# Feed-forward weights' low parts on GpSimd, the last norm by tiles, one weight piece a slot later, and four gaps between tiles

## The reference, cut to what matters

```python
x = _layernorm(x + attn(x, Wq, bq, Wk, bk, Wv, bv, Wo, bo))   # 16 heads, 4 kv heads, rope, causal
x = _layernorm(x + wkv(w, u, x, ctx))                          # a recurrence over the rows
h = silu(x @ rw1.T + rb1)                                      # router, 64 wide
logits = (h @ rw2.T + rb2)[:, :16] + gates                     # top 2 of 16 experts, softmax
base = x @ W.T + bias
delta = einsum(einsum(x, A) * coeff, B)                        # rank 16 for each expert
x = _layernorm(x + base + delta)
```

## Time and profile before

| | |
|---|---|
| three timed runs | 1602.74, 1603.1 and 1606.97 us, median 1603.1 |
| the profiled execution | 1607.82 us, of it span 1606.0 |
| mean granted clock of TensorE | 0.991 |
| TensorE, VectorE, ScalarE, GpSimd busy | 1556.0, 1340.3, 1115.5, 1007.7 us |

### The profile page before, as it was taken

One profiled execution on the slowest core, in us unless ns is written; L12 is line 12 of the kernel. 1 busy time (PEld: TensorE's weight loads), 2 busy tenths in 40 slices (PEclk: granted clock), 3 DMA queues, 4 the chain that ended last, 5 costly groups with the idle time before them and its releaser, 6 DMA issues.

```text
span 1606.0 us, 32704 instructions
## 1 busy us (share of the span) xinstructions
PE 1556.0 (97%) x10500; PEld 1413.4 (88%) x10500; DVE 1340.3 (83%) x3434; ACT 1115.5 (69%) x2995; POOL 1007.7 (63%) x850
## 2 busy tenths in 40 slices
PE   8999999999999999999999999999999987989997
PEld 7899999999999999999999999999999976878785
DVE  6776688889888889898999889898989897877863
ACT  6777787877787778777877787878787865334332
POOL 2665586757675867676767666676667653635653
PEclk9999999999999999999999999999999999999999
DMA  9765344324442444244424442445144522121211
GB/s 298 256 225 201 112 150 137 116 73 142 150 137 55 152 146 136 60 152 151 139 60 152 151 139 60 132 146 164 44 126 148 178 70 79 53 93 66 80 66 53
DMA packets 81625, 202.62 MB, mean 126 GB/s; under 512 B 10416, under 2 KB 11056, under 8 KB 81456
## 3 DMA queue, kind: packets, MB, share of 16 engines
q1 hardware_dynamic: 81456, 200.53, 40.0%
HBM read 120.80 MB, written 37.75 MB: 99 GB/s over the span
## 4 chain that ended last, share of the span: by engine, by line
PE 84%; DVE 7%; issue 3%; POOL 2%; ACT 1%; DVEq 1%; DMA 1%; SPq 0%; ACTq 0%; POOLq 0%
PE bank L528 25%; PE bank L529 24%; PE bank L530 24%; PE bank L652 5%; PE bank L597 2%; PE bank L643 1%; PE bank L598 1%; PE bank L635 1%; DVE PS L1328 1%; DVE ED L1339 1%; PE bank L667 1%; DMA SW<-QB 1%; DVE SW L1392 0%; DVE RC L1170 0%; DVE OTl L1243 0%
## 5 line engine op out<-in xcount | busy, mean ns | idle before, releaser
L528 PE MATMUL bank<-Xh,W 128*128 128x256 f32 x1280 | 362.2, 283 | 5.8 <-DVE RC L1170 2.5
L529 PE MATMUL bank<-Xl,W 128*128 128x256 f32 x1280 | 360.5, 282 | 0.0
L530 PE MATMUL bank<-Xh,W 128*128 128x256 f32 x1280 | 360.4, 282 | 0.0
L1025 POOL TENSOR_TENSOR Ql<-RC,Qh 128x512 fp32r<-128x512 f32 x127 | 169.6, 1336 | 208.9 <-ACT Qh L744 208.7
L759 ACT ACTIVATE S<-S,NM 128x128 f32<-128x128 f32 (+1 forms) x512 | 228.2, 447 | 65.8 <-DVE NM L1155 65.2
L528 PEld LDWEIGHTS bank<-Xh,W 128*128 128x128 f32 x1280 | 241.3, 189 | 9.2 <-DVE RC L1170 5.1
L1013 POOL TENSOR_TENSOR SW<-SW,tables 128x512 f32<-128x512 f32 x128 | 170.8, 1334 | 124.6 <-DMA SW<-QB 124.5
L744 ACT ACTIVATE PTh<-bank 128x384 fp32r<-128x384 f32 x256 | 124.9, 488 | 173.1 <-PE bank L652 173.1
L529 PEld LDWEIGHTS bank<-Xl,W 128*128 128x128 f32 x1280 | 241.7, 189 | 0.0
L530 PEld LDWEIGHTS bank<-Xh,W 128*128 128x128 f32 x1280 | 241.6, 189 | 0.0
L744 ACT ACTIVATE S<-S,RL 128x128 f32<-128x128 f32 (+1 forms) x512 | 203.4, 448 | 31.7 <-DVE RL L1162 31.5
(11 more groups left out here) (161 smaller groups left out, 4450.1 us busy)
## 6 DMA issues: line engine op xcount, KB each, us to landing
W<-kept SPq DMA_DIRECT2D x140, 512.0 KB, 4.5
SW<-QB SPq DMA_DIRECT2D x256, 128.0 KB, 2.3
kept<-W SPq DMA_DIRECT2D x40, 512.0 KB, 5.0
XR<-XR SPq DMA_DIRECT2D x64, 128.0 KB, 2.3
RO<-in_xn SPq DMA_DIRECT2D x16, 512.0 KB, 4.1
KVT<-in_ctxt SPq DMA_DIRECT2D x16, 512.0 KB, 4.2
mixed<-RO SPq DMA_DIRECT2D x16, 512.0 KB, 3.8
XR<-in_xt SPq DMA_DIRECT2D x15, 512.0 KB, 4.2
```

Source lines behind the costliest of these rows:

```text
L528: nc.tensor.matmul(dst, lhs[0], rhs[0], start=first, stop=False)
L529: nc.tensor.matmul(dst, lhs[0], rhs[1], start=False, stop=False)
L530: return nc.tensor.matmul(dst, lhs[1], rhs[0], start=False, stop=last)
L1025: gp.tensor_tensor(Q[1][:, :, :], RC[:, i % 2, :, :], Q[0][:, :, :], ALU.subtract).then_inc(q_lo, 1)
```

## The change

1. Four tiles `gap0` to `gap3` that nobody uses are declared between others: 64 bytes in each partition before X, 64 before K, 64 before Q and 32 before PT. X moves by 64 bytes, K to KRC by 128, Q and S by 192, PT and all behind it by 224.
2. The low parts of the ten feed-forward pieces are subtracted by GpSimd, at the same slots, behind its own `slot(n)` and ahead of its steps.
3. Piece 8 of the first half is copied at slot 2 instead of 1, and its low part made at slot 3 instead of 2, both right ahead of piece 9's.
4. For the last batch the logits are issued in the middle part of step 17, right behind the transposes, and no longer behind `dense(1)`.
5. For the last batch the norm runs tile by tile: VectorE makes the statistics of tile 0 at the end of step 18, as soon as its sum is there, GpSimd's three operations and ScalarE's scaling are done for each tile with a semaphore count of its own, and each tile is stored by itself.

```diff
-SPLIT_AT = [[-6, -6, -2, -2, -6, -6, 0, 1, 1, 2, 3, 4] + [h // 2 + 4 for h in range(HEADS)],
+SPLIT_AT = [[-6, -6, -2, -2, -6, -6, 0, 1, 2, 2, 3, 4] + [h // 2 + 4 for h in range(HEADS)],
...
+        def gap(i, n):
+            sb(f"gap{i}", [P, n // 4])
...
+        gap(0, 64)
         X = [sb(f"X{i}", [P, 2, KC, T], fr) for i in "hl"]
+        gap(1, 64)
...
+        gap(2, 64)
         Q = [sb(f"Q{i}", [P, 2, T], fr) for i in "hl"]
...
+        gap(3, 32)
         PT = [sb(f"PT{i}", [P, 4, P + T], fr) for i in "hl"]
...
                         last.then_inc(hid_turned, 1)
+                        if f == LAST:
+                            logits()
                 else:
                     dense(1)
                     turn_x2(1)
-                    f = stage_of(n, 2)
-                    if f is not None:
...
+                    if stage_of(n, 2) != LAST:
+                        logits()
...
                         for t in range(TT):
+                            act.wait_ge(f_shift, f + 1 + t * (f == LAST))
...
-                        last.then_inc(f_done, 1)
+                            if f == LAST or t == TT - 1:
+                                last.then_inc(f_done, 1)
...
+            def ffn_weights(n):
+                for i in range(NF):
+                    if FFN_SPLIT_AT[i] + 1 == n:
+                        pool.wait_ge(w_hi, HALVES * NP + i + 1)
+                        gp.tensor_tensor(FFN_TO[i][1], ffn_stage(i), FFN_TO[i][0], ALU.subtract).then_inc(w_lo, 1)
...
                     out_sum(3, 0)
+                    if stage_of(n, 3) == LAST:
+                        dve.wait_ge(f_sum, TT * LAST + 1)
+                        dve.wait_ge(f_shift, LAST - 1)
+                        norm_stats(OUT[LAST % 2], LAST % 2, STF, MVF, VEF, f_ve, range(1))
...
-            def ffn_weights(n):
-                for i in range(NF):
-                    if FFN_SPLIT_AT[i] + 1 == n:
-                        dve.wait_ge(w_hi, HALVES * NP + i + 1)
-                        v.tensor_tensor(FFN_TO[i][1], ffn_stage(i), FFN_TO[i][0], ALU.subtract).then_inc(w_lo, 1)
```

More of the change, by code:

```diff
@@ L484, in step @@
                 if f is not None and part == 2:
-                    sp.wait_ge(f_done, f + 1)
-                    sp.dma_start(out[TAIL_BATCH[f], :, :].rearrange("(a p) c -> p a c", p=P), OUT[f % 2]).then_inc(f_out[f % 2], 16)
+                    rows = out[TAIL_BATCH[f], :, :].rearrange("(a p) c -> p a c", p=P)
+                    if f < LAST:
+                        sp.wait_ge(f_done, f + 1)
+                        sp.dma_start(rows, OUT[f % 2]).then_inc(f_out[f % 2], 16)
+                    else:
+                        for t in range(TT):
+                            sp.wait_ge(f_done, f + t + 1)
+                            sp.dma_start(rows[:, t, :], OUT[f % 2][:, t, :]).then_inc(f_out[f % 2], 16)
             def load_piece(u):
@@ L668, in turn_x2, with logits @@
                         last.then_inc(f_turned, 1)
+                def logits():
+                    f = stage_of(n, 2)
+                    if f is not None:
+                        pe.wait_ge(hid_copied, f + 1)
+                        for a in range(TT):
+                            last = nc.tensor.matmul(bank[4][:, T + a * EXP:T + (a + 1) * EXP], HST[:, a * P:(a + 1) * P], Rw2, start=True, stop=True)
+                        last.then_inc(logits_done, 1)
                 def dense(t):
@@ L1258, in odd, with norm_stats @@
                 tail(n, 0)
-            def norm_stats(tiles, par, stats, mv, ve, done):
-                for t in range(TT):
+            def norm_stats(tiles, par, stats, mv, ve, done, which=range(TT)):
+                for t in which:
                     v.bn_stats(stats[:, par, t, :], tiles[:, t, :])
                 dve.drain()
-                for t in range(TT):
+                for t in which:
                     v.bn_aggr(mv[:, par, t, :], stats[:, par, t, :])
                 dve.drain()
-                v.tensor_scalar(ve[:, par, :], mv[:, par, :, 1], EPS, None, ALU.add).then_inc(done, 1)
+                those = slice(which.start, which.stop)
+                v.tensor_scalar(ve[:, par, those], mv[:, par, those, 1], EPS, None, ALU.add).then_inc(done, 1)
             def norm_shift(par, mv, rs, nm):
@@ L1383, in step @@
                         above(dve, f_shift, f - 1)
[L1384 removed]
+                        norm_stats(OUT[f % 2], f % 2, STF, MVF, VEF, f_ve, range(f == LAST, TT))
                     f = stage_of(n, 2)
@@ L1431, in splits @@
                 v.tensor_tensor(w_part(i, 1), stages[u % STAGES], w_part(i, 0), ALU.subtract).then_inc(w_lo, 1)
-            def ffn_weights(n):
-                for i in range(NF):
-                    if FFN_SPLIT_AT[i] + 1 == n:
-                        dve.wait_ge(w_hi, HALVES * NP + i + 1)
-                        v.tensor_tensor(FFN_TO[i][1], ffn_stage(i), FFN_TO[i][0], ALU.subtract).then_inc(w_lo, 1)
-            run(dve, slot, splits, ffn_weights, step, behind=1)
+            run(dve, slot, splits, step=step, behind=1)
 def layouts(i):
```

23 lines of the change are left out of this document (10 added, 13 removed).

## The result

The changed kernel took 1589.4 us (median of four runs, 1587.6 to 1591.5) where the kernel before took 1604.7 on the same chip: ratio 0.9905, 95% interval 0.9884 to 0.9926, so 15 us less (12 to 19). In a later session the same pair gave 1588.8 against 1607.9, 0.9881 (0.9865 to 0.9898). The prediction had 6.1 us less and a range that ended at 1591. Faster was right; the size was not.

What follows compares the result with a forecast made beforehand. TensorE, busy 97% of the span, was taken as the bound, so savings elsewhere count only where it waits. Terms -1.5, -4.9, +0.3 and 0 gave -6.1: 1597.0 us from the median 1603.1, 8 in 10 range 1591 to 1603.

Steps and rivals of the forecast that it cites:

- Part 4: Address gaps before X, K, Q and PT: taken as 0, bounds 5 us less and 11 us more.
- Rival 3: Addresses help: at 1 ns per matmul on X, 5.4 us less, 1591.6 us; chance 0.12.
- Part 2: Kernel end, last batch's logits earlier and norm by tile: 4.9 us less, bounds 2.5 and 5.5.
- the clock term: Matmuls after the last weighted rows: shorter pause, no fall to 1.2 GHz, 1.6 us gained, bounds 0 and 1.7.
- The wait of the logits: Last batch's logits, issued earlier: TensorE idle 0.5 us for ScalarE's copy that they need.
- Rival 2: The clock fall before 1588 returns at another place, so the clock gain doesn't come: 1598.6 us; chance 0.15.
- Part 1: Ten low parts moved from VectorE to GpSimd: 1.5 us less, bounds 3.5 less and 1 more.
- rival 5: Low parts weren't waited for, so moving them gains 0: 1598.5 us; chance 0.06.
- the 0.3 at the hidden layer: Stop of 5.18 us at 1344.47, router's hidden layer: 0.3 us gained, bounds 1.1 gained or lost.
- I charge 0.5: GpSimd's late operations, behind pieces 8 and 9, meet two VectorE scans: 0.5 us lost, bounds 0 and 2.6.
- rival 1: GpSimd holds VectorE at the seam and delays weighted rows: Part 1 becomes +1, 1599.5 us; chance 0.17.
- Part 3: Ninth piece one slot later, near 24 us: 0.3 us more, bounds 0 and 1.1 more.

## Why the prediction was right, and where it was wrong

**What bounds the kernel: right, and it held the warning.** TensorE had no slack in the attention stage, and the text said that all else counts only "if matmuls themselves change speed". They did.

**Part 4, the gaps: the step that failed.** "One per cent lies between them, and it doesn't go with the position ... I take 0." Measured: 13 us (10 to 16) where the bound below ended at 5. Three things were wrong in it. First, compared different shapes and different pairs; X and W were in the trace at one distance only, so no row spoke about another, and the bound of 1 ns had no row under it. Nor does a rule that gives no time say that the time is nothing. Second, I read only the mean duration. It did fall with the spacing (282 to 278), but that matmuls on X could start closer together stood, before the change, only in the distances from start to start, a cycle of 112 to 124. Third, I looked for a position of each tile, modulo 128; what sorts the runs is the place of two tiles to each other. Rival 3 had the direction (the addresses help), with 1 ns on 5376 matmuls where it was 3.7 ns on 3840 and 3.3 on 1536, and a chance of 0.12. Why the distance sets the pace stays open. With 13 in its place the sum would have been 19.1: 1588.8 from the 1607.9 of the second session, which is what the changed kernel took there, and 1585.6 from the 1604.7 of the first, where it took 1589.4.

**Part 2, the end: right, but for what the clock term is worth.** Forecast 4.9; measured 4.5 (2.2 to 5.6) as a time, and 5.4 between the traces of before and of the end alone: 2.0 at the stop (1.8 forecast), 1.6 for the clock (1.6), 1.9 behind (1.5). With the new end the granted clock never fell between the weighted rows and the last matmul, as forecast. But "I keep my part 2 clock term for them too" took the profiled execution for all of them: with the old end the fall is missing in five of eleven. In the mean the term is then some 0.9 (six elevenths of 1.6, an estimate), the sum 4.8, nearer to the measured 4.5. The wait of the logits is 0.47 where 0.5 was worked out. Rival 2's fall in another place didn't come.

**Part 1, the low parts: the sum isn't refuted and isn't shown.** Forecast 1.5; measured 1.4 (0 to 3.1) as a time, and 0.7 from slot 247 to the second weighted rows in the means of seven and eleven traces, with a scatter of 1. Two of the terms are seen in these means: 0.8 up to slot 255, where 0.7 was forecast for pieces 0 and 1 (VectorE's `W` is gone from the chain near slot 254, which speaks against rival 5), and 1.0 up to the first weighted rows, as forecast. The 1.08 by which the stop fell from before to after agrees with it by luck, as this stop is anything from 0.4 to 3.1 with the same code. For the 0.3 at the hidden layer nothing can be said: its first row on VectorE, 1.40 before and 1.29 after, takes 0.29 to 1.40 in the kernels with the low parts on VectorE and 0.29 to 1.31 with them on GpSimd. GpSimd took 1.31 for 512 columns (1.30 forecast) and 0.98 for 320 (0.85). The term that was too small is "I charge 0.5": the way to the second weighted rows gave back the 1.0 and 0.2 more. In four of seven traces that is two scans longer by 1.0 each, of which TensorE had a stop of 0.9 to 1.0, the trigger that was named. It lies within its bounds of 0 and 2.6. The Trainium skill ("SBUF — State Buffer", Who interferes with whom) says that a two-input VectorE instruction and a GpSimd instruction that reads SBUF lock each other out; the two scans of 2.15 and 2.23 us beside GpSimd's bias sums and product, and of 1.22 and 1.20 without them, agree. As rival 1 it had Part 1 at +1, 1 us slower; the low parts alone took 1.4 less, with an interval that ends at 0.

**Part 3, piece 8: the mechanism right, the size too small.** Forecast 0.3, bounds 0 and 1.1; measured 0.8 at slot 7. The 1.0 late at slot 1 came as worked out, and the stop for the swap gave half of it back, as I said; but the same lateness was back at slot 6, and the forecast's rows end at 29 us.

**Adding up.** Without part 4 the forecast was 6.1 less; the run of exactly that took 7.1 less (4.7 to 9.2). Of the 19 us that TensorE saved on matmuls, 6.6 turned into waits, nearly all for VectorE. No part of the forecast had that term: with TensorE faster, VectorE's share of the chain rose from 7% to 16%.

## What to carry to other kernels

A change of addresses is a change of speed until a run says otherwise: where one engine is busy all of a stage, a few bytes in front of a tile that it streams are worth trying, and a single gap (with a second one that puts the rest back) shows which tile it is. Read the pace of a pipelined engine from start to start as well as from the duration of one instruction: some of the distances before were as short as the best ones after, which showed that there was something to gain. And compare a stop over several traces before a difference of 1 us is put down to an edit. When a row is missing, the nearest rows bound a cost only if they differ from it in nothing but that one thing.

## What the hardware showed that I had not expected

- Matmuls that stream X (256 columns, 1024 bytes a partition) past W start mostly 113 to 114 ns apart when X begins 192 bytes behind W modulo 256, 117 to 118 at 64, 120 at 0, and 112 to 124 in a cycle at 128. While X is streamed the next part of W is being loaded (PEld is busy 88% of the span beside TensorE's 97%), so both may meet in the same part of the memory. That explanation is only argued: no run took either away, and W against OT, K against Q and P against V with 512 columns didn't follow the table's order.
- W against OT: 232.2 to 233.1 ns at a distance of 32, 229.4 and 229.5 at 64 (230.9 where X isn't moved), 233.8 to 234.6 at 96, 232.1 at 192.
- With the same stop of 2.4 us before it and the same instructions behind it, the clock of the last dense half fell to 1.2 GHz in six traces of eleven and not in the others.
- The same kernel twice had different stretches at half clock (1.2 GHz) in the seam. The window there of the changed kernel, first and second time (granted clock in the column behind the busy time):

```profile
1299.00:1338.00 39.00, 29.43 (x146) 0.82 0.30 95
```

```profile
1299.00:1338.00 39.00, 30.76 (x163) 0.91 0.31 95
```

  Its logits of batch 0 came 2.2 us later in the first, after allowing for the 0.7 it was late at slot 247. This is as large as parts 1 and 3 together, and the reason why their sizes are read from stretches of several traces beside the times.

What remains best is the changed kernel with piece 8 at slot 1 (ratios to before 0.9883 and 0.9867, where the changed kernel itself has 0.9905 and 0.9881); the two were not separated by more than their intervals.
